# Four f32 projections of a fused attention and channel-mixing kernel, rewritten as three f16 products each

## The reference

```
x = x + layernorm(attn(layernorm(x)))
x = x + layernorm(ffn(layernorm(x)))

attn: q, k, v = x @ Wq, x @ Wk, x @ Wv   (16 heads of 16; q / 4)
      q_l, k_l = means of q and k over 64 groups of 32 tokens (landmarks)
      s1 = softmax(q k_l^T), s2 = softmax(q_l k_l^T), s3 = softmax(q_l k^T)
      out = (s1 @ (pinv(s2) @ (s3 @ v))) @ Wo + bo      (pinv: six iterations)
ffn:  x_prev = x shifted by one token
      xr = mu_r * x + (1 - mu_r) * x_prev,  xk likewise with mu_k
      r = sigmoid(xr @ W_r^T),  k = xk @ W_k^T
      out = r * (relu(k)^2 @ W_v^T)
```

## Time and profile before

| | |
|---|---|
| time, median of 3 runs | 1839.56 us (1833.84 to 1845.88) |
| the profiled execution, from its first to its last instruction | 1835.2 us |
| TensorE, VectorE, ScalarE, POOL busy | 1572.9, 1383.5, 1013.7, 275.4 us |
| mean granted TensorE clock | 0.936 of full speed |
| first part | to about 390 us |

### The profile page before, as it was taken

How to read it: one execution, slowest core, us unless ns; L and a number is a source line. 1 busy time by engine, 2 the same in 40 slices (tenths; PEclk the granted TensorE clock), 3 DMA queues, 4 the chain that set the end, 5 groups by cost and what they waited for, 6 DMA issues and landing times. The chain is left out here.

```text
span 1835.2 us, 50877 instructions
## 1 busy us (share of the span) xinstructions
PE 1572.9 (86%) x21132; PEld 1089.9 (59%) x21132; DVE 1383.5 (75%) x3089; ACT 1013.7 (55%) x1642; POOL 275.4 (15%) x163
## 2 busy tenths in 40 slices
PE   4878888977698998898989989898999889988785
PEld 3678778963545655565557456655655564556453
DVE  6799889977468947876796689579867966894565
ACT  1589768952454465456536544655565365535442
POOL 5200020000001111121011111111210111111212
PEclk7789989998999999999999999999999999989897
DMA  7400110022211213121222122131212221121001
GB/s 229 139 11 4 63 45 4 4 63 53 63 44 40 70 45 93 35 68 51 68 60 69 53 53 71 46 93 34 68 54 67 61 68 53 50 53 40 28 33 35
DMA packets 125844, 104.67 MB, mean 57 GB/s; under 512 B 30512, under 2 KB 123568, under 8 KB 125616
## 3 DMA queue, kind: packets, MB, share of 16 engines
q1 hardware_dynamic: 125616, 101.42, 19.7%
HBM read 56.23 MB, written 19.92 MB: 41 GB/s over the span
## 5 line engine op out<-in xcount | busy, mean ns | idle before, releaser
L964 ACT ACTIVATE p<-wide 128x1024 f32<-128x1024 f32 x128 | 124.0, 1021 | 119.1 <-PE wide L1736 118.0
L1796 PE MATMUL bank<-wrT,xrT 128*128 128x256 f32 x512 | 146.8, 450 | 46.0 <-ACT vv L930 36.1
L1285 DVE TENSOR_REDUCE m<-wide 128x16 f16<-128x1024 f32 x128 | 150.4, 1216 | 40.8 <-PE wide L1620 40.5
L941 ACT ACTIVATE e<-wide 128x1024 f32<-128x1024 f32 x128 | 124.5, 1021 | 81.4 <-PE wide L1653 70.2
L1796 PEld LDWEIGHTS bank<-wrT,xrT 128*128 128x128 f32 x512 | 114.7, 229 | 73.2 <-issue 40.1
L1277 DVE TENSOR_REDUCE m<-wide 128x2 f32<-128x1024 f32 x128 | 149.8, 1213 | 2.9 <-PE wide L1600 2.9
L790 POOL TENSOR_TENSOR ob<-ob,xm 128x1024 f32<-128x1024 f32 x32 | 77.0, 2405 | 472.9 <-DVE ob L398 472.9
L1776 PE MATMUL bank<-wo,oT 128*128 128x256 f32 x512 | 120.9, 390 | 6.2 <-DVE xT L1245 3.6
L1806 PE MATMUL acc<-xkT,wkT 128*128 128x512 f32 x256 | 120.0, 613 | 7.1 <-DVE xkT L1358 7.1
L784 POOL TENSOR_TENSOR xkT<-x2T 128x1024 f32<-128x1024 f32 x32 | 60.6, 1892 | 431.9 <-ACT x2T L989 431.9
L774 POOL TENSOR_TENSOR xm<-yy,xres 128x1024 f32<-128x1024 f32 x32 | 76.1, 2378 | 314.5 <-DVE yy L398 164.6
(11 more groups left out here) (286 smaller groups left out, 3756.7 us busy)
## 6 DMA issues: line engine op xcount, KB each, us to landing
x1in<-in_L_attn_x SPq DMA_DIRECT2D x8, 2048.0 KB, 8.3
xin<-in_L_attn_x SPq DMA_DIRECT2D x32, 512.0 KB, 4.1
k_stack<-kh SPq DMA_DIRECT2D x256, 64.0 KB, 2.0
xres<-in_L_attn_x SPq DMA_DIRECT2D x32, 512.0 KB, 4.0
out<-ob SPq DMA_DIRECT2D x32, 512.0 KB, 5.1
k_stack<-kl SPq DMA_DIRECT2D x128, 64.0 KB, 2.0
q_stack<-landmarks SPq DMA_DIRECT2D x192, 4.0 KB, 1.7
inverse<-X SPq DMA_DIRECT2D x8, 256.0 KB, 2.0
```

The lines of the kernel that those rows point to most:

```text
L941: sc.activation(e3[w][:, :], wide[w][:, :], ACT.Exp).then_inc(wide_drained[w], 1)
L964: sc.activation(p1[:, 2 * j:2 * j + 2, :], wide[w][:, :].rearrange("p (a n) -> p a n", a=2), ACT.Exp).then_inc(wide_drained[w], 1)
L1285: v.tensor_reduce(m1[:, tiles, 2 * w:2 * w + 2, :].rearrange("p t q x -> p q t x"), wide[w][:, :].rearrange("p (q t x m) -> p q t x m", q= ...
L1796: ins = mm(bank[j][:, t * A:(t + 1) * A], xrT[:, k, tok], wrT[:, k, :], start=(k == 0), stop=(k == KB - 1))
```

## The change

Weights: w2 holds high and low f16 parts of Wo, W_r, W_k and W_v, times 16 (WS). ScalarE makes the high parts; VectorE makes Wo's low part, POOL those of the other three at the end of its work in the first part. Activations: oT (scaled by OS = 64 through wbd), xrT, xkT and ka (scaled by KAS squared) are cast to f16 by ScalarE, and VectorE subtracts to get the low part, in the new stages OH (o16), TH (xr16, xk16) and KA (ka16; its cast is in ScalarE's share of GK). O, GR, GK and G2 on TensorE run the six f16 products of TERMS in place of two f32 products, and wait for the low parts. The scales are taken out in instructions that were there. XA normalises x in xin itself; xhat and its wait are gone, and the load X now waits for R of the chunk that used the buffer. In V the products run pair by pair, the two halves in turn.

```diff
-        wo = sb("wo", [P, KB, A])
-        wrT = sb("wrT", [P, KB, A])
-        wkT = sb("wkT", [P, KB, A])
-        wvT = sb("wvT", [P, KB, A])
+        OS, KAS = 64.0, 4.0
+        w2 = sb("w2", [P, 4, 2, KB, A], F16)
...
-        xhat = [sb(f"xhat{i}", [P, NT, A], c=part2) for i in range(2)]
...
+        o16 = sb("o16", [P, 2, KB, CH], F16, c=part2)
+        xr16 = sb("xr16", [P, 2, KB, CH], F16, c=part2)
+        xk16 = sb("xk16", [P, 2, KB, CH], F16, c=part2)
+        ka16 = sb("ka16", [P, 2, KB, CH], F16, c=part2)
...
-        BODY = [("C1", 2, 0), ("R", 3, 0), ("GK", 1, -1), ("C2", 2, 0), ("O", 3, -1), ("B2", 2, 0), ("T", 2, -1),
+        BODY = [("C1", 2, 0), ("R", 3, 0), ("GK", 1, -1), ("C2", 2, 0), ("KA", 1, -1), ("O", 3, -1), ("B2", 2, 0),
...
             def stage_X(at, b, c):
                 if b > 0 or c >= 2:
 
-                    sp.wait_ge(x_applied, b * NC + c - 1)
+                    u = (at["R", c - 2] if c >= 2 else at["R", c + 2, 1]).bank
+                    for k in range(KB):
+                        sp.wait_ge(bank_full[k], u + 1)
...
+            pool.wait_ge(w2_hi, 4)
+            for w in range(3):
+                g.tensor_tensor(w2[:, 1 + w, 1, :, :], wt[w][:, :, :], w2[:, 1 + w, 0, :, :],
+                                ALU.subtract).then_inc(w2_lo, 1)
...
+            sc.activation(w2[:, 0, 0, :, :], wo[:, :, :], ACT.Copy, scale=WS).then_inc(w2_hi, 1)
+            act.wait_ge(wT_drained, 3)
+            for w in range(3):
+                sc.activation(w2[:, 1 + w, 0, :, :], wt[w][:, :, :], ACT.Copy).then_inc(w2_hi, 1)
...
+            def stage_OH(at, b, c):
+                n = b * NC + c
...
+                for k in range(KB):
+                    act.wait_ge(acc_drained[k], at["H", c].acc + 1)
+                sc.activation(o16[:, 0, :, :], oT[:, :, :], ACT.Copy).then_inc(o_hi, 1)
+
+            def stage_TH(at, b, c):
...
+                act.wait_ge(xr_made, n + 1)
+                sc.activation(xr16[:, 0, :, :], xrT[:, :, :], ACT.Copy).then_inc(xr_hi, 1)
+                act.wait_ge(xk_made, n + 1)
+                sc.activation(xk16[:, 0, :, :], xkT[:, :, :], ACT.Copy).then_inc(xk_hi, 1)
...
                 sc.activation(ka[:, :, :], ka[:, :, :], ACT.Square).then_inc(ka_made, 1)
+                act.wait_ge(ka_made, b * NC + c + 1)
+                sc.activation(ka16[:, 0, :, :], ka[:, :, :], ACT.Copy).then_inc(ka_hi, 1)
...
+            def stage_OH(at, b, c):
+                dve.wait_ge(o_hi, b * NC + c + 1)
+                v.tensor_tensor(o16[:, 1, :, :], oT[:, :, :], o16[:, 0, :, :], ALU.subtract).then_inc(o_lo, 1)
+
+            def stage_TH(at, b, c):
+                n = b * NC + c
+                dve.wait_ge(xr_hi, n + 1)
+                v.tensor_tensor(xr16[:, 1, :, :], xrT[:, :, :], xr16[:, 0, :, :], ALU.subtract).then_inc(xr_lo, 1)
+                dve.wait_ge(xk_hi, n + 1)
+                v.tensor_tensor(xk16[:, 1, :, :], xkT[:, :, :], xk16[:, 0, :, :], ALU.subtract).then_inc(xk_lo, 1)
+
+            def stage_KA(at, b, c):
+                dve.wait_ge(ka_hi, b * NC + c + 1)
+                v.tensor_tensor(ka16[:, 1, :, :], ka[:, :, :], ka16[:, 0, :, :], ALU.subtract).then_inc(ka_lo, 1)
...
+            def by_token(j, act16, w):
+                for t in range(2):
+                    tok = slice((2 * j + t) * P, (2 * j + t + 1) * P)
+                    for i, (k, wt, xt) in enumerate(TERMS):
+                        ins = mm(bank[j][:, t * A:(t + 1) * A], act16[:, xt, k, tok], w2[:, w, wt, k, :],
+                                 start=(i == 0), stop=(i == len(TERMS) - 1))
+                ins.then_inc(bank_full[j], 1)
...
             def stage_GR(at, b, c):
                 u, n = at["GR", c].bank, b * NC + c
-                pe.wait_ge(xr_made, n + 1)
+                pe.wait_ge(xr_lo, n + 1)
```

More of the change, by code:

```diff
@@ L125, in sandwich @@
         gcol = [sb(f"gcol{s}", [P, PAIRS], c=part1) for s in ROWS]
+        wo = sb("wo", [P, KB, A], c=part1)
+        wt = [sb(f"wt{w}", [P, KB, A], c=part1) for w in range(3)]
         XS, ZS, SS = 64.0, 16.0, 16.0
@@ L440, in sandwich @@
         xk_made = sem("xk_made")
+        o_hi = sem("o_hi")
+        o_lo = sem("o_lo")
+        xr_hi = sem("xr_hi")
+        xr_lo = sem("xr_lo")
+        xk_hi = sem("xk_hi")
+        xk_lo = sem("xk_lo")
+        ka_hi = sem("ka_hi")
+        ka_lo = sem("ka_lo")
         sg_ln = sem("sg_ln")
@@ L1085, in step_pw @@
                                                op0=ALU.mult, op1=ALU.subtract).then_inc(w16_lo, 1)
+                    dve.wait_ge(w2_hi, 1)
+                    v.scalar_tensor_tensor(out=w2[:, 0, 1, :, :], in0=wo[:, :, :], scalar=WS, in1=w2[:, 0, 0, :, :],
+                                           op0=ALU.mult, op1=ALU.subtract).then_inc(w2_lo, 1)
             def step_stl(n):
@@ L1219, in stage_XA @@
             def stage_XA(at, b, c):
-                if b or c >= 2:
-                    u = (at["R", c - 2] if c >= 2 else at["R", c + 2, 1]).bank
-                    for k in range(KB):
-                        dve.wait_ge(bank_full[k], u + 1)
                 dve.wait_ge(x_in[c % 2], 16 * (b * 2 + c // 2 + 1))
                 for t in range(NT):
-                    ins = v.tensor_scalar(xhat[c % 2][:, t, :], xin[c % 2][:, t, :], mv1[b][:, c * NT + t, 0:1],
+                    ins = v.tensor_scalar(xin[c % 2][:, t, :], xin[c % 2][:, t, :], mv1[b][:, c * NT + t, 0:1],
                                           rstd1[b][:, c * NT + t:c * NT + t + 1], ALU.subtract, ALU.mult)
@@ L1554, in stage_R @@
                     for t in range(NT):
[L1555 removed]
+                        ins = tr(bank[k][:, t * P:(t + 1) * P], xin[c % 2][:, t, k * P:(k + 1) * P], ident[:, :])
                     ins.then_inc(bank_full[k], 1)
@@ L1696, in stage_V @@
                 hold(pe)
-                for j in range(2):
-                    r = slice(j * HALF, (j + 1) * HALF)
-                    for a in range(PAIRS):
+                for a in range(PAIRS):
+                    for j in range(2):
+                        r = slice(j * HALF, (j + 1) * HALF)
                         ins = mm(bank[j][r, a * HS:(a + 1) * HS], zt[r, a, :], un[r, a, :], start=True, stop=True)
-                    ins.then_inc(bank_full[j], 1)
+                        if a == PAIRS - 1:
+                            ins.then_inc(bank_full[j], 1)
             def stage_D(at, b, c):
@@ L1811, in stage_G2 @@
                 u, n = at["G2", c].bank, b * NC + c
-                pe.wait_ge(ka_made, n + 1)
+                pe.wait_ge(ka_lo, n + 1)
                 for j in range(2):
                     pe.wait_ge(bank_drained[j], u)
-                    for t in range(2):
-                        tok = slice((2 * j + t) * P, (2 * j + t + 1) * P)
-                        for k in range(KB):
-                            ins = mm(bank[j][:, t * A:(t + 1) * A], ka[:, k, tok], wvT[:, k, :], start=(k == 0),
-                                     stop=(k == KB - 1))
-                    ins.then_inc(bank_full[j], 1)
+                    by_token(j, ka16, 3)
             part2_program(pe, {"R": stage_R, "AQ": stage_AQ, "AK": stage_AK, "AV": stage_AV, "B1": lambda at, b, c: row_maxima(at, b, c, 0),
```

82 lines of the change are left out of this document (46 added, 36 removed), and 78 rows, old and new, of tables (BODY, LAST, PRO).

## The result

The changed kernel takes 2027.0 us (median of 4 runs, 2023.1 to 2033.2) against 1841.3 for the kernel before: ratio 1.102, interval 1.099 to 1.106. The forecast was 1957, with a range up to 2005: the sign was right, the size 70 us short.

The account below looks back on a forecast made before the run. TensorE and its handoffs were taken to bound a cycle's first half, VectorE the second. First cycle 10, six cycles 96, tail 12 sum to 118 on 1835.2: 1953, with 4.4 for the median 1957 us; range 1860 to 2005.

Parts of the forecast that it names:

- upper walk: One cycle, all steps' lateness added along the queues, no gap used twice: 20.8 us a cycle, the upper bound.
- (a): ka16 of chunk 2 ahead of the C1 reduction, G2 waiting for it: first FS 1.1 us late.
- (b): TH of chunk 3: casts and subtractions delay GR, TensorE idle over 3 us; the stretch behind is 4.2 us late.
- (c): KA of chunk 3 directly ahead of the C2 reduction: that reduction 7.2 us late, 6.3 after G2 gives 0.9 back.
- (d): OH 0 and OH 1 ahead of the C1 reduction and O's bias: 1.2 us each, 8.7 late in all.
- (e): TH 0: two casts ahead of norm_y's root, two subtractions ahead of the yy rows: 2.6 us, 11.3 late in all.
- (f): OH 2 ahead of the C1 reduction, VectorE waits for the cast and subtracts: 2.4 us; E1 of chunk 3 13.7 late.
- I take 16: Lateness chosen for a full cycle, 16 us, between bounds 8.4 and 20.8, as VectorE is already 90% busy in 890 to 970.
- lower bound: Per cycle: (a) to (c) 6.3, 850 to 890 gains 1.9, ten later subtractions less VectorE's 8.0 idle us add 4.0: 8.4 us.
- rival of chance 0.15: Contention at shared SBUF, 3.7 us a cycle, and TensorE half clock after waits, 5.6: 1983 to 1996, both 2022; chance 0.15.
- faster: Subtractions fall into VectorE's 40 idle us a cycle, casts done before VectorE comes to them: 1809 us; chance 0.10.
- no change: Half of the handoffs hidden and product time gained balance: 1825 to 1855 us; chance 0.07.

Follow-up runs that it names:

- e13: e1 plus sixteen VectorE subtractions a cycle of the change's size and places, on constant tiles, with no waits to or from them; 1889.2 us, 1.028 of before.
- e3: The changed kernel without its subtractions: casts stay, low parts are zeros written once, waits go by the high part; 1843.9 us, 1.003 of before.
- e16: The changed kernel with ten dummy products into the stage's own bank tile ahead of the low-part wait in GR 3 and O 1; 1992.4 us.
- e1: The changed kernel without its casts and subtractions: the f16 products run on constant tiles, released as the f32 ones were; 1791.5 us, 0.976 of before.
- e5: The changed kernel with O, GR, GK and G2 in f32, without OH, TH, KA; the rest of the change stays; 1831.4 us, 0.997 of before.
- e14: The changed kernel with all casts, places and waits, but each subtraction covers only 8 of 512 columns; 1914.9 us, 1.042 of before.
- e17: The changed kernel with KA 3, TH 0, OH 2 and OH 3 moved behind the reductions in the list, OH 0 left; 1968.7 us, 1.071 of before.

## Why the prediction was wrong

The forecast's sum was 118 us over the span of 1835.2; the profiled executions are 196 apart. The seven cycles gave 169 where 106 were taken, the tail 19 where 12 were, the stretch ahead of them 9 where 0 was. So the miss is in the cycle: 24.1 us where 16 stood. The walk along the queues named the right places and its upper sum, 20.8, was the nearer one. Lateness in the cycle from 853.43, which is 53.10 later than that of the trace before, beside the forecast's upper walk:

| step | forecast late | measured late |
|---|---|---|
| (a) first FS | 1.1 | 1.6 |
| (b) behind GR 3 | 4.2 | 6.6, with 2.4 of half clock |
| (c) FS 5 (829.21 before, 891.72 now) | 7.2 | 9.4 |
| E1 of chunk 0; (d) E1 of chunk 1 | 6.3; 7.5 | 8.7; 10.2 |
| (d) E1 of chunk 2, behind O 1 | 8.7 | 13.6, with 2.5 more of half clock |
| (e) yy rows | 11.3 | 16.2 |
| (f) E1 of chunk 3 | 13.7 | 18.6 |
| end of the cycle | 20.8 | 24.7 |

The difference is 2.2 to 2.7 behind GR 3 and 4.9 from O 1 on, two stages at half clock; it is 3.9 at the end.

- **The first failed step: "I take 16"** between 8.4 and 20.8. The lower bound let VectorE's idle time cover subtractions. e13 shows how little it covers: 4.2 of 18.0 us a cycle even when the subtractions wait for nothing and nothing waits for them. With the waits nothing was covered (24.2 a cycle from e3 to the change), since the idle time stands ahead of an instruction that waits for its cast, and VectorE's idle time grew. The walk named each wait; there was no row for the discount. The upper bounds, by the prediction's own sum, give 1994.
- **The second failed step: the clock was put into a rival of chance 0.15**, at nothing in the sum, though it hangs on waits which the forecast had as certain; the earlier trace rows showed the price. It was priced at 5.6 us a cycle, for the waits of (b) and (f). GR 3 of (b) did fall to half clock; the other stage was O 1, behind the wait of (d), and GR of chunk 2, at full clock before, took 4.2 to 4.4 us in six of the seven cycles. Filling the waits of GR 3 and O 1 gave 4.5 back (e16). The same 12250 matmul records take 978.6 us in e1's seven cycles and 1047.2 in the change's, 9.8 us a cycle more; how much of that lies on the path beyond e16's 4.5 is open. Forecast and rival were not alternatives: they add up. That 1994 + 39 = 2033 lies so near to 2027 is in part luck, as the places differ and the tail is above its bound.
- **Contention**, the rival's other half, was sized from L1358's mean of 0.859 us, 20% over its least. Four of its 64 rows make that mean, 1.9 to 2.8 us long and all after 1635, each beside a POOL addition; the others have 0.74. The contention that came did not fall on the subtractions: mean 1.22 to 1.23, longest 1.77. It fell on POOL's ob addition, for which none of the five engines' rows waits.
- **TensorE's gain** was sized right as work (141 busy us a cycle in e1 for the 139 forecast), and without the handoffs worth 6.0 us a cycle, 40 in the program (e5 to e1). GR's part of it was eaten by half clock (147.1 us).
- **The tail** gained 18.7 for a forecast of 12 (6 to 15). Against e1 it is 32.1 longer: casts and waits show 19.6 of that (e14), VectorE's work alone nothing (e13), and 12.5 appear only with both.
- **Before 466, V's order and x in place**: 0 was taken, and e5 has it (0.997 of before, 0.994 to 1.000).
- **The rivals "faster" and "no change"** fell by their own condition: the casts are not done when VectorE comes to the subtractions; it waits 62 us for ka's alone.

Left open: whether work and waits together cost more than their sum, and why. The medians say 14 us, hardly clear of noise; the profiled executions have 2.1 a cycle and 12.5 in the tail. TensorE's busy time in the seven cycles is also 2.0 a cycle above what e13 and e14 add to e1's, which points at the clock, but no run separates it. Open too is why a wait of 2.26 us ahead of O 1 leaves TensorE at full clock in most cycles of e17 and in none of the changed kernel.

## What to carry to other kernels

Replacing a TensorE product by a cheaper one with a preparation on two other engines is to be costed by the handoff, not by the work: here 40 us of gain stood against 236 of casts, subtractions and waits. Where queues run in order, walk each queue once with the wait in place and believe that sum; idle time pays for new work only if it stands behind the work's own wait. What a wait does to the clock of the next product belongs in the same sum, not beside it. When a stage moves, move its share on every engine, and look at what each share now stands ahead of.
